# A two-layer recurrent, attention and mixture-of-experts kernel on one core: table copies, weight loads, dense product, token ranks and plan moved; warm matmuls left out in one place and put in at another

## The reference, cut to what matters

```
layer 0: attn: y=LN(xn); q,k,v,g = y@W+b; state = decay*state + k*v; out = g*q*state; @Wo; + gelu(LN(..)@W1)@W2
         ffn:  h = silu(xn@w1)*(xn@w2); h = gelu(h@h1); h = gelu(h@h2)   # h2: 512x512, ternary weights
               return (h @ w3) * s                                       # 512 -> 128
layer 1: attn: gated linear attention, 4 heads, chunks of 64, RMS norm of the output, gate, @Wo
         ffn:  softmax attention of 16 heads of 8 features; LN; key = x@router + b;
               expert = floor(key) mod 4; y = relu(x@W1[e]+b1[e])@W2[e]+b2[e]; LN(x + y)
```

## Time and profile before

| what | value |
|---|---|
| median of 3 runs | 2771.05 us |
| lowest, highest | 2768.88, 2776.47 us |
| the profiled execution | 2765.3 us, its span 2763.5 us |
| mean granted TensorE clock | 0.949 of full |
| PE, DVE, ACT, POOL busy | 88%, 70%, 49%, 21% of the span |
| layer 0 | 0 to about 974 us |
| constants | about 977 to 986 us |
| attention | about 986 to 2597 us |
| experts | about 2597 to 2763.5 us |

### The profile page before, as it was taken

How to read it: one execution, slowest core, us unless ns; L and a number is a source line. 1 busy time by engine, 2 the same in 40 slices (tenths; PEclk the granted TensorE clock), 3 DMA queues, 4 the chain that set the end, 5 groups by cost and what they waited for, 6 DMA issues and landing times. The chain is left out here.

```text
span 2763.5 us, 45274 instructions
## 1 busy us (share of the span) xinstructions
PE 2440.8 (88%) x14654; PEld 1702.0 (62%) x14654; DVE 1946.9 (70%) x3706; ACT 1345.7 (49%) x1926; POOL 591.6 (21%) x630
## 2 busy tenths in 40 slices
PE   3899999999999858889988998899888988999496
PEld 2778888888888645555555545555445545554396
DVE  3789888888888513667767777777777777672275
ACT  1444444444444312366566656666565656555142
POOL 0111112111211100111212222222222231212177
PEclk9999999999999878999999999999999999998698
DMA  5443432242232133432344323432343333301373
GB/s 153 128 124 106 130 93 74 82 136 78 74 103 80 43 138 89 119 95 75 100 127 117 89 79 114 133 91 75 100 133 100 81 102 88 85 28 37 114 236 107
DMA packets 194686, 280.31 MB, mean 101 GB/s; under 512 B 21576, under 2 KB 151065, under 8 KB 185760
## 3 DMA queue, kind: packets, MB, share of 16 engines
q1 hardware_dynamic: 189088, 266.47, 32.6%
q0 software_dynamic: 5504, 12.63, 1.3%
HBM read 148.65 MB, written 131.91 MB: 102 GB/s over the span
## 5 line engine op out<-in xcount | busy, mean ns | idle before, releaser
L1578 DVE TENSOR_REDUCE c_row_max<-b_psum 128x2 f32<-128x1024 f32 x512 | 624.9, 1220 | 283.6 <-PE b_psum L1287 281.0
L1425 ACT ACTIVATE c_prob<-b_psum 128x1024 f32<-128x1024 f32 x512 | 525.6, 1027 | 376.6 <-PE b_psum L1305 371.7
L1305 PE MATMUL b_psum<-c_cq,c_ck 25*128 25x512 f32 x1024 | 262.5, 508 | 76.6 <-ACT c_prob L1425 72.8
L1287 PE MATMUL b_psum<-c_bk,c_bq 24*128 24x512 f32 x1024 | 263.9, 511 | 64.2 <-DVE c_row_max L1578 54.8
L1315 PE MATMUL b_psum<-c_prob,c_v_aug 128*32 128x512 f32 x2048 | 287.0, 634 | 0.1
L1305 PEld LDWEIGHTS b_psum<-c_cq,c_ck 25*128 25x128 f32 x1024 | 96.8, 186 | 255.3 <-ACT c_prob L1425 149.2
L353 PE MATMUL a_psum<-a_yT_hi,a_w_hi 128*128 128x512 f32 x512 | 205.7, 402 | 9.1 <-issue 5.9
L353 PE MATMUL a_psum<-a_yT_hi,a_w_lo 128*128 128x512 f32 x512 | 203.2, 397 | 0.0
L353 PE MATMUL a_psum<-a_yT_lo,a_w_hi 128*128 128x512 f32 x512 | 202.8, 396 | 0.0
L1287 PEld LDWEIGHTS b_psum<-c_bk,c_bq 24*128 24x128 f32 x1024 | 97.6, 187 | 104.7 <-DVE c_row_max L1578 87.3
L459 ACT ACTIVATE a_g<-a_psum,a_cols 128x512 f32<-128x512 f32 x64 | 44.1, 690 | 238.3 <-PE a_psum L353 234.6
(11 more groups left out here) (296 smaller groups left out, 5562.2 us busy)
## 6 DMA issues: line engine op xcount, KB each, us to landing
sorted_scratch<-a_pad SPq DMA_DIRECT2D x16, 2184.5 KB, 14.4
g_scratch<-a_g_hi SPq DMA_DIRECT2D x16, 1024.0 KB, 4.0
g_scratch<-a_g_lo SPq DMA_DIRECT2D x16, 1024.0 KB, 7.2
c_g_hi<-g_scratch SPq DMA_DIRECT2D x16, 1024.0 KB, 5.8
c_g_lo<-g_scratch SPq DMA_DIRECT2D x16, 1024.0 KB, 7.9
stack_scratch<-c_qk_hi SPq DMA_DIRECT2D x256, 64.0 KB, 1.6
d_wt<-expert_scratch SPq DMA_DIRECT2D x19, 834.0 KB, 5.6
c_bq<-stack_scratch SPq DMA_DIRECT2D x128, 96.0 KB
```

What stands on the lines that cost most here:

```text
L1287: mm = nc.tensor.matmul(psum[:, MAX + x, :], bq[r, j, cut(t)], bk[r, j, :], start=True, stop=True)
L1305: mm = nc.tensor.matmul(psum[:, SCORE + x, :], ck[r, j, cut(kb)], cq[r, j, :], start=True, stop=True)
L1425: nc.scalar.activation(prob[:, i % 4, :, :], psum[:, SCORE:SCORE + 2, :], ACT.Exp, scale=DH1 ** -0.5).then_inc(S["exp"], 1)
L1578: nc.vector.tensor_reduce(row_max[:, t, at:at + 3:2], psum[:, MAX:MAX + 2, :], AX.X, ALU.max).then_inc(S["row_max"], 1)
```

## The change

1. In layer 0 the twelve table copies are no longer issued in one burst. Two of them follow each of the last six `prep_st`.
2. `f_hi` and `f_lo` are loaded in four parts each, at the start of round -3 of the attention stretch, behind the first load of g1; TensorE waits for part c where `h2` first uses it.
3. `few` leaves out round -2: its 80 warm matmuls go.
4. In the attention round `w3` comes in four quarters at p23, p25, p27 and p30, `x1` at p31, `rank` at p30, `slot` at p31, and `osquare` and `gate` at p23.
5. The 15 operations of the plan stand at the end of the attention's DVE program, in tiles that the attention already has; SP no longer waits for a plan in the experts.
6. Four 128x512 matmuls whose result nobody reads stand ahead of TensorE's first work in the experts.
7. The last `root` stands behind the stores of group 17.

```diff
@@ layer 0, SP
-                        if n == PREP_PER_ROUND and kind == "prep_ld":
-                            for d, plain in table_parts:
-                                sp.dma_start(d, plain).then_inc(S["table_out"], 16)
...
                         elif kind == "prep_st":
                             sp.wait_ge(S["prep_lo"], n + 1)
                             sp.dma_start(dst, prep[:, :, 0:width].bitcast(F32)).then_inc(S["prep_out"], 16)
+                            if n >= len(prep_chunks) - len(table_parts) // 2:
+                                at = 2 * (n - len(prep_chunks) + len(table_parts) // 2)
+                                for d, plain in table_parts[at:at + 2]:
+                                    sp.dma_start(d, plain).then_inc(S["table_out"], 16)
@@ attention_order
-    put(25, "C2", "rank")
-    put(26, "C2", "slot")
+    put(30, "C2", "rank")
+    put(31, "C2", "slot")
...
-    put(24, "A1", "osquare", 0)
-    put(24, "A1", "gate")
+    put(23, "A1", "osquare", 0)
+    put(23, "A1", "gate")
...
-    put(24, "F", "w3", 0)
-    put(26, "F", "w3", 1)
-    put(27, "F", "x1")
...
+    for t, p in enumerate(W3_AT):          # W3_AT = (23, 25, 27, 30)
+        put(p, "F", "w3", t)
+    put(31, "F", "x1")
@@ attention
-            few = r in (-2, -1) or BATCH - 3 <= r < BATCH
+            few = r == -1 or BATCH - 3 <= r < BATCH
...
+            def dense_weights():
+                for c in range(HID):
+                    at = slice(HID * c * P, (HID * c + HID) * P)
+                    for part, dst in enumerate((f_hi, f_lo)):
+                        sp.dma_start(dst[:, at].bitcast(F32), d_f[:, part, at]).then_inc(f_loaded[c], 16)
...
                 if isinstance(base, int) and add == -3:
+                    dense_weights()
                     rest_of_weights()
@@ attention, PE
+                        if not looped and add == -3:
+                            pe.wait_ge(f_loaded[c], 32)
...
-                        for t in (2 * i, 2 * i + 1):
-                            for k in range(HID):
-                                mm = nc.tensor.matmul(bank("w3")[:, cut(t)], h2g[:, k, cut(t)], w_block(f_w3, k),
-                                                      start=(k == 0), stop=(k == HID - 1))
-                        if i:
+                        for k in range(HID):
+                            mm = nc.tensor.matmul(bank("w3")[:, cut(i)], h2g[:, k, cut(i)], w_block(f_w3, k),
+                                                  start=(k == 0), stop=(k == HID - 1))
+                        if i == TILES - 1:
                             mm.then_inc(filled, 1)
...
-            pe.wait_ge(f_loaded, 32)
             run(pe, rounds)
@@ attention, DVE (the 15 operations of the plan, from experts)
             run(dve, rounds)
+            nc.vector.memset(plan_ones[:, :], 1.0).then_inc(S["plan_step"], 1)
+            dve.wait_ge(S["place"], BATCH)
+            nc.vector.tensor_tensor(plan_count[:, :], place[:, :], place0[:, :], ALU.subtract).then_inc(S["plan_step"], 1)
...
+            nc.vector.tensor_copy(plan_i[:, :, :], plan[:, :, :]).then_inc(S["plan_i"], 1)
@@ experts, SP and PE
-            sp.wait_ge(S["plan_i"], 1)
...
+            for n in range(4):
+                nc.tensor.matmul(psum[:, Y[1], :], ident[:, :], rows[:, 0:TILES, :].rearrange("p n d -> p (n d)"), start=True, stop=True)
             turn(0)
@@ experts, POOL
-                if k + 1 < GROUPS:
+                if k + 2 < GROUPS:
                     root(k + 1)
... (the four indirect stores of group k)
+                if k + 2 == GROUPS:
+                    root(k + 1)
@@ constants, SP
-                for part, dst in enumerate((f_hi, f_lo)):
-                    sp.dma_start(dst[:, :].bitcast(F32), d_f[:, part, :]).then_inc(f_loaded, 16)
```

More of the change, by code:

```diff
@@ L975, in attention, with plan_tile @@
         slot_i = sb("slot_i", [P, TILES], I32)
+        plan_at = iter(range(0, SEQ, TILES * GROUPS + TILES))
+        def plan_tile(*shape):
+            first, n = next(plan_at), shape[0] * (shape[1] if len(shape) > 1 else 1)
+            view = qg[:, first:first + n]
+            return view if len(shape) == 1 else view.rearrange("p (a b) -> p a b", b=shape[1])
+        plan_ones, plan_number = (kg[:, GROUPS * i:GROUPS * i + GROUPS] for i in range(2))
+        plan_count, plan_groups, plan_ends, plan_jump = (kg[:, 2 * GROUPS + EXPERTS * i:2 * GROUPS + EXPERTS * (i + 1)] for i in range(4))
+        plan_over, plan_past, plan_shift = plan_tile(EXPERTS, BATCH), plan_tile(GROUPS, EXPERTS), plan_tile(GROUPS, EXPERTS)
+        plan_shift_sum = plan_tile(GROUPS)
         PV, SCORE, MAX, FFN, RING = 0, 2, 4, (1,), (6, 7)
@@ L1733, with experts @@
 T_ROW = T_B2 + P
-def experts(nc, psum, ident, rows, minus_half, eps, place, place0, d_sorted, d_table, d_out):
+def experts(nc, psum, ident, rows, minus_half, eps, plan_i, d_sorted, d_table, d_out):
     with ExitStack() as ctx:
@@ L1750, in experts @@
         XB, WB, OB = 5, 4, 4
-        ones = sb("ones", [P, GROUPS])
-        number = sb("number", [P, GROUPS])
-        count = sb("count", [P, EXPERTS])
-        over = sb("over", [P, EXPERTS, BATCH])
-        groups = sb("groups", [P, EXPERTS])
-        ends = sb("ends", [P, EXPERTS])
-        past = sb("past", [P, GROUPS, EXPERTS])
-        jump = sb("jump", [P, EXPERTS])
-        shift = sb("shift", [P, GROUPS, EXPERTS])
-        shift_sum = sb("shift_sum", [P, GROUPS])
-        plan = sb("plan", [P, 2, GROUPS])
-        plan_i = sb("plan_i", [P, 2, GROUPS], I32)
         xt = [sb(f"xt{n}", [P, TILES, PAY]) for n in range(XB)]
@@ L1885, in _ @@
-            have = count[:, :].unsqueeze(2).to_broadcast([P, EXPERTS, BATCH])
-            nc.vector.scalar_tensor_tensor(out=over[:, :, :], in0=step, scalar=float(SEQ), in1=have, op0=ALU.mult,
-                                           op1=ALU.is_lt).then_inc(S["steps"], 1)
-            dve.wait_ge(S["steps"], 4)
-            nc.vector.tensor_reduce(groups[:, :], over[:, :, :], AX.X, ALU.add).then_inc(S["steps"], 1)
-            dve.wait_ge(S["steps"], 5)
-            nc.vector.tensor_tensor_scan(ends[:, :], ones[:, 0:EXPERTS], groups[:, :], 0.0, ALU.mult, ALU.add).then_inc(S["steps"], 1)
@@ L2057, in layer1 @@
         psum = ctx.enter_context(nc.psum_tensor("b_psum", [P, 8, BANK], F32))
-        f_loaded = ctx.enter_context(nc.semaphore("b_f_loaded"))
+        f_loaded = [ctx.enter_context(nc.semaphore(f"b_f_loaded{c}")) for c in range(HID)]
         b_loaded = ctx.enter_context(nc.semaphore("b_b_loaded"))
```

71 lines of the change are left out of this document (39 added, 32 removed).

## The result

| | before | after |
|---|---|---|
| median of 4 runs, us | 2771.94 (2768.88 to 2776.47) | 2741.42 (2737.27 to 2744.39) |
| ratio | | 0.9882 (0.9860 to 0.9904) |
| profiled execution, us | 2765.3 | 2737.3 |
| its span, us | 2763.5 | 2735.4 |
| mean granted clock | 0.949 | 0.954 |

The kernel is 1.2% faster. The direction and most terms were right. Two terms were mis-sized, with opposite signs: the table copies gave 3 us instead of 6.5, the order of the attention round about 10 instead of 5. Some 6 us more came in the last round, by its clock, from a cause that stays open.

What follows compares the result with a forecast made beforehand. The prediction saw TensorE as the bound in layer 0, trading with VectorE and ScalarE in attention, with DMA and GpSimd chains elsewhere. Its terms summed to -22.6 us, from 2771.05 to 2748.5 us, range 2733 to 2765.

Steps and rivals of the forecast that it cites:

- table copies: Layer 0: without the burst, chunk 4's load issues earlier and ScalarE's 6.1 us wait goes; -6.5 us.
- warm matmuls, round -2: Start of attention: removal lets queries, keys and the first maximum start earlier; -7.4 us, bounds -10.5 and -2.
- order: Attention rounds: moved operations take VectorE work from between row maxima and spread matmuls; -0.35 a round, -5 us over 14.
- those loads have some 10 us in hand: Layer 0: later chunk loads can absorb delay by copies, since 14.2 us of delay cost only 6.1.
- the loss of 2: Layer 0: lower bound for the table copies; two copies behind each later store could make next loads late, 2 us lost.
- upper bound of 8.9: Layer 0: most the table copies could gain, the burst round's whole excess, 63.3 - 54.4 = 8.9 us.
- the instructions alone are worth -0.2 a round: Attention loop: reordering at full clock shortens p22 to p31 from 25.8 to 25.4 us, with 0.1 to 0.3 given back.
- the clock is worth more: Attention loop: more evenly spread matmuls gain a tenth of the 1.5 us tied to second half-clock stretches.
- Rival A: Attention p27 to p31: new 3 us idle drops the clock every round; +34 instead of -5, 2787 us; chance 0.12.
- Rival D: Round -2's clock falls (7.4 becomes 2) and paired copies delay loads (6.5 becomes 2); 2758.5 us; chance 0.14.
- B: Attention loop stays as it is, 0 instead of -5, as only order moves; 2753.5 us; chance 0.20.
- C: Attention loop: even order removes the second half-clock stretches, -21 instead of -5; 2732 us; chance 0.14.

Runs made afterwards that it cites:

- e7: Changed kernel with the twelve table copies again in one burst ahead of prep chunk 4: 2745.40 us, ratio 0.9898 to the old kernel.
- e8: Changed kernel with the table copies ahead of layer 0's last but one round and the last root ahead of group 17's stores: 2735.68 us, ratio 0.9857.
- f4: Changed kernel with the dense weights again in two 1 MB loads in the block of constants: 2737.24 us, ratio 0.9909.
- e6: Changed kernel with the 80 warm matmuls of round -2 back: 2748.03 us, ratio 0.9914.
- e1: Changed kernel with its whole attention round put back to the old order: 2752.67 us, ratio 0.9973.
- f1: Changed kernel with only rank and slot back at p25 and p26: 2743.60 us, ratio 0.9929; twelve loop rounds 1071.48 us.
- f2: Changed kernel with w3 in halves and x1, osquare and gate at their old places, rank and slot still late: 2733.97 us, ratio 0.9899; loop 1058.28 us.
- e2: Changed kernel without the four warm matmuls ahead of the experts: 2739.23 us, ratio 0.9929.
- e3: Changed kernel with the last root back ahead of group 17's stores: 2735.13 us, ratio 0.9922.
- e5: The old kernel once more, unedited: 2770.52 us in one run; twelve loop rounds 1077.59 us, last round 63.78 us.

## Why the prediction was right, and where it was wrong

| term | forecast | measured | from |
|---|---|---|---|
| table copies | -6.5 | -2.9 | layer 0, e7, e8 |
| dense weights | -1.5 | -1.0 | stage; f4 shows 0.7 |
| warm matmuls, round -2 | -7.4 | -8.1 | stage; e6 shows 6.9 |
| order | -5 | -10 | e1, f1, f2 |
| plan | -3 | -2.8 | first token load |
| four matmuls | -0.5 | -1.3 | e2 |
| last root | +1.3 | +1.7 | e3 |
| clock in the last round | none | -5.8 | e1, e5; cause open |
| sum | -22.6 | -30.2 | span -28.1 |

**Table copies, mis-sized.** The mechanism held: e7 brings the wait of 6.1 us back. The step that failed is "those loads have some 10 us in hand": it holds where a copy costs 0.6 to 0.7 us of issue, but behind the 2.2 MB store the load's own issue grows from 3.6 to 5.4 us with the copies ahead of it, and ScalarE waits 2.7 us for it. I had the bound for it (the loss of 2) and took it as unlikely. A second slip has no effect on the sum: of the idles in the burst's round, the longest of TensorE, 5.9 us, is there in both kernels, with the same length:

```profile
127.57 0.77 PE L354 MATMUL a_psum<-a_yT_hi,a_w_hi 128*128 128x512 f32 x1 [5.92 <-issue]
```

The upper bound of 8.9, the whole excess over a steady round, was therefore never to be had; the half clock that follows this idle stays too.

**Order, mis-sized, and my account of it wrong in both parts.** I wrote "the instructions alone are worth -0.2 a round". f2 at equal clock shows -1.0. I had counted the slot's 1.8 us as leaving, and then let w3's quarters and the wait at p27 take it back; and I had not asked why one multiply of 16 elements takes 1.15 us in a row of 0.17s, which is time that vanishes and isn't moved. It stood in my own timeline. And I wrote "the clock is worth more": it was worth nothing. The loop's mean granted clock is 0.96 in before, e5, e1 and after alike, and the 7.3 us between e1 and after come at that same clock. Moving rank and slot gives -13.4 in the loop with w3 in halves (f2 against e1), the quarters behind it about +6.6. Rival A had the place and the mechanism of that loss (a new idle at p27, then half clock, in every round), but an idle of 3 us where 1.19 and 0.46 stand, and a price of 2.4 us a round where 0.5 was measured. Of the -10, the loop's -8.9 are shown by e1 and f1, whose loops are back at the old time. The -2.7 of rounds 13 and 14 are in e1 (179.80) but not in f1 (176.25), so they don't belong to rank and slot alone; single executions vary there (e8, in the new order, has 179.89). The last round gives back 1.4 (e1, f1). The +1.6 of rounds -1 and 0 varies from execution to execution and is in no row of the table.

**Round -2** went as worked out (6.9 us for 7.4), with other waits than mine (0.87 for VectorE's x instead of a third copy). Rival D, with the clock falling here, is refuted by the window at 1.00; its other half, the delayed loads, is what happened to the copies.

**Plan, dense weights, matmuls, last root** were each within 0.8 us. For the four matmuls "a little sooner" was too little: the first products of the experts run at full clock (0.73 before, 1.00 after).

So the total was right to 8 us partly by luck: I had 3.6 us too much for the copies and 5 too little for the order, which offset, and nothing for the 5.8 of the last round. B is refuted by the loop, C by its clock: no round of after's loop is without a second stretch.

## What to carry to other kernels

Look for the instruction that takes several times as long as others of its size on the same engine, and see what runs beside it: moving it can make time vanish, where moving normal work only shifts it. When a burst of transfers is spread, list what already stands at each new place; the price is set by the worst of them. Whether filler work for the clock pays must be asked round by round, since dropping the same eighty matmuls won 6.9 us in one round and lost 10.4 in the next. Undo each part by itself and look at every stage: e1 and f1 showed that a gain of the last round, which I had put down to the order, was not its own.
